# A transformer layer on one core: a matmul of constants repeated on TensorE ahead of the last four tiles

## What is computed

```python
def _L0_attn_ref(x, ...):
    x = x + _gdn(_layernorm(x, ln1_g, ln1_b), Wq, Wk, Wv, Wb, Wg, Wo, bo)
    h = _layernorm(x, ln2_g, ln2_b)
    h = gelu(h @ w1 + b1) @ w2 + b2
    return x + h

# _gdn: 16 heads of 16, a recurrence over the 512 positions
def step(Sst, inp):
    q_t, k_t, v_t, b_t, g_t = inp
    Sst = Sst * g_t[..., None, None]
    kS = einsum('bhk,bhkv->bhv', k_t, Sst)
    Sst = Sst + b_t[..., None, None] * einsum('bhk,bhv->bhkv', k_t, v_t - kS)
    o_t = einsum('bhk,bhkv->bhv', q_t, Sst)
    return (Sst, o_t)
# out = out @ Wo + bo

xn = _layernorm(x)
x = x + _L0_attn_ref(xn, ...) + _L0_ffn_ref(xn, ...)   # 64 experts, top 8, and a shared one
```

## Time and profile before

| | us |
|---|---|
| median of 3 runs | 1930.82 (1924.5 to 1932.3) |
| profiled execution | 1931.82 |
| its span, first to last instruction | 1930.1 |
| TensorE busy | 1436.1 (74%) |
| VectorE busy | 1742.8 (90%) |
| GpSimd busy | 1587.7 (82%) |
| ScalarE busy | 909.1 (47%) |

### The profile page before, as it was taken

How to read it: one execution, slowest core, us unless ns; L and a number is a source line. 1 busy time by engine, 2 the same in 40 slices (tenths; PEclk the granted TensorE clock), 3 DMA queues, 4 the chain that set the end, 5 groups by cost and what they waited for, 6 DMA issues and landing times. The chain is left out here.

```text
span 1930.1 us, 31359 instructions
## 1 busy us (share of the span) xinstructions
PE 1436.1 (74%) x8802; PEld 1247.6 (65%) x8802; DVE 1742.8 (90%) x4967; ACT 909.1 (47%) x2609; POOL 1587.7 (82%) x1343
## 2 busy tenths in 40 slices
PE   6776777877854577667665668988898988789738
PEld 5665666766743566556554557877777877668637
DVE  3599999999999999999987988989999999988970
ACT  4545455556544644555542445555554454334303
POOL 5469999898998888788897788889898999897851
PEclk9878778878875788788776779999999999989868
DMA  8575345534456657855658322242223311111120
GB/s 174 149 178 116 69 97 125 133 75 96 95 124 150 155 132 164 217 132 130 165 132 222 74 61 64 84 118 69 57 60 102 87 54 49 57 50 49 40 53 13
DMA packets 337169, 201.24 MB, mean 104 GB/s; under 512 B 208227, under 2 KB 327717, under 8 KB 336997
## 3 DMA queue, kind: packets, MB, share of 16 engines
q1 hardware_dynamic: 318724, 168.43, 35.5%
q0 software_dynamic: 15616, 30.55, 7.2%
q10 hardware_dynamic: 2656, 0.26, 0.1%
HBM read 127.58 MB, written 71.60 MB: 103 GB/s over the span
## 5 line engine op out<-in xcount | busy, mean ns | idle before, releaser
L827 POOL TENSOR_TENSOR rp<-S,qs 128x2048 f32<-128x2048 f32 x113 | 519.8, 4600 | 89.3 <-DVE S L1138 63.7
L1123 DVE SCALAR_TENSOR_TENSOR vwin<-S,gwin,bank 128x256 f32<-128x256 f32 x1024 | 483.7, 472 | 0.3
L1138 DVE SCALAR_TENSOR_TENSOR S<-S,gwin,bank 128x256 f32<-128x256 f32 x1024 | 483.1, 472 | 0.3
L1128 DVE TENSOR_REDUCE nu<-vwin 128x16 f32<-128x272 f32 x1024 | 438.1, 428 | 0.3
L1132 DVE TENSOR_TENSOR bank<-nu,bank 128x256 f32<-128x256 f32 x1024 | 430.6, 421 | 0.6
L1773 PE MATMUL bank<-region 128*128 128x128 f32 x2048 | 288.2, 301 | 0.0
L1773 PEld LDWEIGHTS bank<-region 128*128 128x128 f32 x2048 | 273.1, 214 | 18.7 <-issue 18.0
L835 POOL TENSOR_TENSOR r<-rp 128x1024 f32<-128x1024 f32 x113 | 274.3, 2428 | 7.0
L1653 PE MATMUL bank<-xaT,wqkvg 128*128 128x128 f32 (+1 forms) x1792 | 242.1, 288 | 11.1 <-ACT xaT L1312 8.0
L1784 PE MATMUL bank<-region 128*128 128x256 f32 x1024 | 234.7, 383 | 0.0
L1653 PEld LDWEIGHTS bank<-xaT,wqkvg 128*128 128x128 f32 (+1 forms) x1792 | 216.2, 190 | 25.5 <-ACT xaT L1312 11.6
(11 more groups left out here) (158 smaller groups left out, 2329.6 us busy)
## 6 DMA issues: line engine op xcount, KB each, us to landing
qkv_d<-stg SPq DMA_DIRECT2D x192, 128.0 KB, 2.3
region<-in_L_ffn_w_gate SPq DMA_DIRECT2D x64, 192.0 KB
region<-in_L_ffn_w_up SPq DMA_DIRECT2D x64, 192.0 KB
region<-in_L_ffn_w_down SPq DMA_DIRECT2D x64, 192.0 KB
region<-in_L_attn_x SPq DMA_DIRECT2D x16, 512.0 KB, 7.6
region<-in_L_attn_x SPq DMA_DIRECT2D x32, 256.0 KB, 4.8
xw_d<-region SPq DMA_DIRECT2D x32, 256.0 KB, 3.5
acc_d<-region SPq DMA_DIRECT2D x32, 256.0 KB, 4.1
```

Source lines behind the costliest of these rows:

```text
L827: g.tensor_tensor(rp[:, :, :].rearrange("p (a v) d -> p a v d", v=DH), S[h][:, lo:lo + HS].rearrange("p t s (v d) -> p (t s) v d", v=DH), ...
L1123: m[G] = mark(v.scalar_tensor_tensor(products_of(I, s, G)[0], earlier(h, s, G).rearrange("p (v d) -> p v d", v=DH), gwin[:, I // NB2 & 1, ...
L1128: m[G] = mark(v.tensor_reduce(nu[:, G], products_of(I, s, G)[1], AX.X, ALU.add))
L1138: ins = v.scalar_tensor_tensor(S[h][:, s, G], earlier(h, s, G), gwin[:, I // NB2 & 1, G, 1, t:t + 1], outer[G], ALU.mult, ALU.subtract)
```

## The change

On TensorE's queue, between the last of the 64 iterations and the tail, TensorE waits until the last GELU of tile LAST - 1 is done and until step 3 of the last iteration of the recurrence is done. Then it multiplies wo_s[:, 0, :] (128x256) by ident 70 times into bank G0, waits until the outputs of the last part are stored, does the same matmul 8 times more, and goes on with the tail as before. The results are overwritten and used by nobody. Nothing is changed on the other engines.

```diff
                 if I == ROUNDS_END + 2:
                     mlp_bias_mm()
+            def keep_running(n):
+
+                for _ in range(n):
+                    mm(G0[:, 0:D], ident[:, :], wo_s[:, 0, :], start=True, stop=True)
+
+            pe.wait_ge(gelu_done, LAST * 2 + 1)
+            pe.wait_ge(rec_done, 2 * NT + 1)
+            keep_running(70)
+            pe.wait_ge(o_stored, OST * (NBLK - 1 + PARTS))
+            keep_running(8)
             back_attn(LAST)
             back_attn(LAST + 1)
             back_T(LAST)
```

## The result

The changed kernel takes **1941.12 us** (median of 5 runs, 1940.66 to 1945.42) against 1929.72 us before (5 runs, 1924.5 to 1932.3). The ratio is **1.0059, 95% interval 1.0044 to 1.0074**: slower by 0.6%. Forecast were 1941.0 us and slower by 0.53%.

What follows compares the result with a forecast made beforehand. The tail was taken as bound by TensorE, some 19 us of it at half clock. A start 13.4 us late, less 3.0 and 0.6 us regained, gave +9.8 us: 1941.0 us, 0.53% slower, eight-in-ten range 1935 to 1944.5.

Steps and rivals of the forecast that it cites:

- The start: Before the tail: the filler starts at 1855.7, when the last recurrence state is ready, on a clock already down for 2 us.
- The length of the filler: TensorE ahead of the tail: 78 matmuls at 0.4325 us plus 2.8 us lost end at 1892.3, delaying attention products 13.4 us.
- the slow start: First 5.6 us of filler run at half clock, losing 2.8 us (bounds 1.75 and 4.3).
- The attention products at full clock: Start of the tail: the two attention products take 3.4 us instead of 6.4, gaining 3.0 us.
- The clock over the gap: Between second and third attention products: the clock falls again despite a transpose, so the third runs at half clock.
- the first rival: Gap after the second attention product: clock stays up, gaining 4.3 us behind it; +6.1 us in all, 1937.3 us; 10%.
- The half-clock stretch behind it: Third attention product and MLP in the tail: 7.5 us at half clock against 8.6, gaining 0.6 us (bounds 0 and 1.3).
- The sum: Whole tail: +13.4 - 3.0 - 0.6 = +9.8 us, bounds +8.0 and +11.9.
- (1): Gap after the second attention product: clock stays up, +6.1 us in all, 1937.3 us, no measurable difference; 10%.
- (2): Filler ahead of the tail: repeats cost one record, 0.216 us, so it ends before the data come; 1924 to 1927 us; 4%.
- (3): Filler ahead of the tail: never gets the clock up, all 78 at half clock, 44 us late, 1975 us; 2%.
- (4): Recurrence beside the filler: slowed, but a shift up to 13 us stays hidden; result as forecast, no chance of its own.

Runs made afterwards that it cites:

- e5_longer: The changed kernel with 94 instead of 70 matmuls before the wait for the stored outputs; one execution, 1955.3 us.
- e1_short: The changed kernel with 38 instead of 70 matmuls before the wait, the 8 behind it kept; 1924.11 us, ratio to before 0.9974.
- e2_short_gap: e1_short plus 4 matmuls between the second attention product and the transpose and 2 behind the transpose; 1924.32 us, ratio to before 0.9959.
- e3_long_gap: The changed kernel with 70 and 8 kept, plus 4 matmuls before the transpose and 2 behind it; 1938.07 us, ratio to before 1.0039.
- e6_bridge: The changed kernel without the 70, 4 instead of 8 behind the wait, plus 4 before the transpose and 2 behind it; 1923.71 us, ratio to before 0.9962.
- e7_fit: e2_short_gap with 7 instead of 8 matmuls behind the wait for the stored outputs; 1924.45 us, ratio to before 0.9964.
- e4_gap_only: The kernel before plus only 2 matmuls between the second attention product and the transpose and 1 behind the transpose; 1928.69 us, ratio to before 0.9985.

## Why the prediction was right, point by point

**The start.** Forecast 1855.7, at the mark; measured 1854.69 with the mark at 1854.67. Right.

**The length of the filler.** Forecast 30.3 + 2.8 + 3.5 = 36.6 us, measured 36.02. The price of one, 0.4325 us taken from L1784, holds: 0.427 by the difference to e5_longer. What the term was too high by comes from the slow start: the clock came back after 4.3 us instead of 5.6, which is 0.65 us less lost. This term was mis-sized by that much, within its bounds. The first product started 36.0 us after the mark instead of 23.2: 12.8 us late, forecast 13.4.

**The attention products at full clock.** From the first product to the third it is 1897.93 - 1890.71 = 7.2 us, against 1889.16 - 1878.92 = 10.2 before: 3.0 us gained, as forecast.

**The clock over the gap.** Forecast was that it falls; it fell, 2.6 us after the last attention product, with one transpose in the gap. The guidance of the Trainium skill (TensorE: Matmul & The Clock Gate, Why this matters for your kernels), to avoid idle gaps of over about 3 us, would have called gaps of 2.18 and 1.43 us with a transpose between them safe. They were not: the clock was down 2.6 us after the last product here, and in e1_short after 1.7 us, inside the first gap of 2.18 us. At the refill, whose gap of 3.64 us is longer than that figure, it was down after 2.4 us. e2_short_gap and e3_long_gap show that the gap is the cause: filled, the clock stays up, and the third product and what follows gain 3.75 and 4.2 us, where the first rival had put 4.3.

**The half-clock stretch behind it.** Forecast 7.5 us against 8.6 before, a gain of 0.6. Measured 1897.93 to 1906.7, 8.8 us, a gain of none. This gain was put 0.6 us too high, which balances the slow start's term. In e1_short the same stretch is 7.9 us and in e5_longer 8.6, so it varies by about what the three rows had shown; that the two misses cancel is luck.

**The sum.** 12.8 - 3.0 + 0.0 = +9.85 us in the tail measure, forecast +9.8. The medians differ by 11.4 us; the 1.5 us between lie within the spread of the runs, as those of before cover 7.8 us. So the agreement of the forecast time, 1941.0 us, with the measured 1941.12 is closer than the reasoning can claim: it was reckoned from a median of before of 1930.8 us, and the median of before over 5 runs is 1929.72. The forecast of slower by more than 0.5% came down on the right side of an edge that it had called even, and the interval of the ratio, 1.0044 to 1.0074, still includes that edge; that much was luck.

**The rivals.** The clock did not stay up over the gap (1). A repeat of the same constants was not cheaper (2): there are 156 records, at 0.43 us a pair. The filler did not stay at half clock (3): the clock was up after 4.3 us. The recurrence was not slowed (4): the loads were issued 19.8 us after the mark, as before.

## What to carry to other kernels

A filler has to be shorter than the idle time it fills, counted at its price at both clocks: past the arrival of the data every matmul is paid in full, while full clock gives back only half of the work that it reaches. Put it last before the data and into the small gaps of the chain behind, not first into the long wait: ten matmuls placed so (e6_bridge) gave 0.4% here, 52 with most of them in the long wait (e2_short_gap) gave the same, and 78 too long cost 0.6%. When the effect is smaller than the spread of whole executions, compare the profiles from a fixed event to the end.

## What the runs showed of the hardware that I had not expected

How soon the clock came back after TensorE began to work varied with what it did. With a stream of filler matmuls it was 3.5 us in e6_bridge (1874.25 to 1877.8) and 4.0 to 4.5 us in the six kernels with a filler in the long wait: 4.3 in the changed one (1854.7 to 1859.0), 4.5 in e1_short (1853.97 to 1858.5), 4.0 in e7_fit (1852.52 to 1856.55). With attention products first, which include the products of one row, it was 8.6 us in the kernel before, counted from the third product, and 11.8 us in e4_gap_only, counted from the first (1880.70 to 1892.5), though TensorE was busy for 11.38 of 11.70 us there. Why is open: no run here separates the products of one row from the short idle times. In the kernel before, idle time within the stretch can't be the reason, since TensorE is busy for all of its 8.64 us.

How soon the clock fell after the last attention product varied too, for gaps that are alike: 1.7 us in e1_short, 2.4 in e5_longer, 2.6 in the changed kernel.

Three matmuls in a gap were worth 3.4 us on a clock that was down already (3.6 us less the 0.2 us by which the loads came sooner). The expectation had been 1 to 3. In that kernel the clock came back 36.0 us before the end of the span, in the kernel before 32.3 us: here a filled gap hastened the rise, as in four other profiles it prevented the fall. The earlier rise is seen in one profile; the ten runs, at a ratio of 0.9985 (0.9971 to 0.9998), agree with a gain but do not size it.
